# An empty half position in each gate chunk, and the last expert groups mixed straight from PSUM

## What is computed

```python
edge_index = jnp.stack([src, dst])
x = x + gnn(layernorm(x), edge_index, ...)            # attention over 212500 edges
x = x + ffn(layernorm(x)[None], ...)[0]
# ffn: gates from a graph attention over 131072 + 12500 edges, 4 heads x 4 experts
h = (x_flat @ W_gat).reshape(M, HEADS, NUM_EXPERTS)
alpha = softmax over the edges of a node of leaky_relu(a_src[src] + a_dst[dst], 0.2)
agg = segment_sum(h[src] * alpha[:, :, None], dst) + b_gat
scores = layernorm(agg, ln_gamma, ln_beta).reshape(M, HEADS, NUM_EXPERTS).mean(1)
w = softmax(top_k(scores, 2))
for ei in range(NUM_EXPERTS):
    hh = gelu(x @ W1[ei] + b1[ei], approximate=False)
    out = out + g[..., None] * (hh @ W2[ei] + b2[ei])
```

## Time and profile before

| | us |
|---|---|
| median of 3 runs | 5126.29 |
| lowest and highest of them | 5109.45, 5126.61 |
| profiled execution, its own time | 5112.58 |
| span of the profile, first to last instruction | 5110.8 |

### The profile page before, as it was taken

How to read it: one execution, slowest core, us unless ns; L and a number is a source line. 1 busy time by engine, 2 the same in 40 slices (tenths; PEclk the granted TensorE clock), 3 DMA queues, 4 the chain that set the end, 5 groups by cost and what they waited for, 6 DMA issues and landing times.

```text
span 5110.8 us, 56011 instructions
## 1 busy us (share of the span) xinstructions
PE 3488.7 (68%) x13829; PEld 2416.2 (47%) x13829; DVE 3343.7 (65%) x7445; ACT 2023.4 (40%) x5460; POOL 3027.1 (59%) x3037
## 2 busy tenths in 40 slices
PE   0443346566666665666665658898888988898995
PEld 0332223333333333333333328777766767676874
DVE  8988966666666666666555556265656666665478
ACT  0321145566565665566665656222222222221121
POOL 0000077777777777777777740777777777776001
PEclk9876677877888788787787875899999999999897
DMA  3111144333333333333444447322222222221079
GB/s 117 66 48 43 50 112 105 105 102 103 103 103 103 103 102 102 99 97 103 106 106 106 106 122 246 91 45 45 43 64 43 47 41 43 43 47 40 28 296 357
DMA packets 273867, 489.23 MB, mean 96 GB/s; under 512 B 78747, under 2 KB 174438, under 8 KB 267292
## 3 DMA queue, kind: packets, MB, share of 16 engines
q0 software_dynamic: 128928, 271.00, 22.2%
q1 hardware_dynamic: 144636, 214.78, 12.0%
HBM read 368.67 MB, written 116.87 MB: 95 GB/s over the span
## 4 chain that ended last, share of the span: by engine, by line
DVE 28%; PE 25%; POOL 24%; issue 12%; DVEq 5%; ACT 4%; DMA 2%; SPq 0%; POOLq 0%
POOL MEM L611 23%; PE ps L1606 16%; DVE MEM L1200 6%; DVEq L1187 4%; DVE MEM L864 2%; DVE MEM L866 2%; PE ps L1672 2%; PE ps L1660 2%; ACT hot L710 2%; POOL MEM L598 2%; PE ps L1636 1%; DVE MEM L877 1%; DVE MEM L1030 1%; DVE MEM L878 1%; PE ps L1548 1%
## 5 line engine op out<-in xcount | busy, mean ns | idle before, releaser
L598 POOL DMA_INDIRECT MEM<-h_table,MEM x1856 | 1818.5, 980 | 1171.7 <-DVE MEM L980 606.6
L1606 PE MATMUL ps<-MEM,hot 128*128 128x257 f32 x3712 | 1372.9, 485 | 367.4 <-DVE MEM L1200 293.7
L611 POOL DMA_INDIRECT MEM<-gate_table,FI x1122 | 1167.9, 1041 | 525.6 <-issue 341.6
L1200 DVE SCALAR_TENSOR_TENSOR MEM<-MEM,FI,ps 128x257 f32 x1856 | 894.3, 482 | 722.9 <-PE ps L1606 442.6
L1606 PEld LDWEIGHTS ps<-MEM,hot 128*128 128x128 f32 x3712 | 725.1, 228 | 958.8 <-ACT hot L710 521.1
L710 ACT ACTIVATE hot<-hot,FI 128x128 f32<-128x128 f32 x1856 | 889.1, 479 | 2.2
L689 ACT ACTIVATE hot<-iota_row,FI 128x128 f32<-128x128 f32 x1856 | 736.0, 397 | 372.6 <-PE ps L1606 348.7
L1660 PE MATMUL ps<-MEM 128*128 128x256 f32 x3136 | 768.3, 401 | 26.1 <-DMA MEM<-xT_tiles 26.1
L1672 PE MATMUL ps<-MEM 128*128 128x256 f32 x3136 | 743.0, 391 | 7.3 <-ACT MEM L750 7.3
L750 ACT ACTIVATE MEM<-ps,b_cols 128x256 f32<-128x256 f32 x784 | 324.6, 472 | 961.9 <-PE ps L1660 961.7
L1660 PEld LDWEIGHTS ps<-MEM 128*128 128x128 f32 x3136 | 616.7, 201 | 122.5 <-issue 22.2
(11 more groups left out here) (284 smaller groups left out, 3174.2 us busy)
## 6 DMA issues: line engine op xcount, KB each, us to landing
y_rows<-MEM SPq DMA_DIRECT2D x196, 256.0 KB, 2.1
MEM<-y_rows SPq DMA_DIRECT2D x49, 1024.0 KB, 7.6
MEM<-h_table,MEM POOLq DMA_INDIRECT x1856, 2.8
h_table<-MEM SPq DMA_DIRECT2D x196, 128.5 KB, 2.7
MEM<-gate_table,FI POOLq DMA_INDIRECT x1122
x_rows<-MEM SPq DMA_DIRECT2D x14, 896.0 KB, 6.7
xT_tiles<-MEM SPq DMA_DIRECT2D x14, 896.0 KB, 4.2
MEM<-xT_tiles SPq DMA_DIRECT2D x98, 128.0 KB
```

Source lines behind the costliest of these rows:

```text
L598: pool.indirect_dma_start(rings[c % 2][:, j, :], None, h_table, bass.IndirectOffsetOnAxis(ap=GI.bitcast(I32)[:, q:q + 1], axis=0)).then_in ...
L611: pool.indirect_dma_start(GR[:, c % GATE_RING, j, :], None, gate_table, bass.IndirectOffsetOnAxis(ap=FI.bitcast(I32)[:, q:q + 1], axis=0)) ...
L1200: dve.scalar_tensor_tensor(target, target, falls[:, p, j:j + 1], ps[:, at:at + ROW], ALU.mult, ALU.add).then_inc(added, 1)
L1606: pe.matmul(ps[:, at:at + ROW], hot[:, q % HOTS, :], rings[p][:, j, :], start=True, stop=True).then_inc(summed, 1)
```

## The change

`ITEMS` becomes 19: a chunk has one more half position, position 4, at which nothing is done, between step 3 and step 4. The steps behind it come half a slot later. Since 19 is odd, chunks with an even number have step 3 on half 0, and chunks with an odd number have it on half 1. `SUMS_AT` becomes 346 (slot 173), and the constants behind it follow: `MIX_LOADS_AT` 176, `SQRT_AT` 176, `TOP_AT` 179, `GATES_BY` 178, `MIX_FROM` 179, `LATE` 45.

Groups 0 to 44 go through `y_rows` and the mixes as before. Groups 45 to 48 (slots 180 to 195) don't: their x1 rows are loaded at slot 178, TensorE adds the bias b2 with one more matmul for each tile, and VectorE's `late_mix` adds the gated result from PSUM to the x1 rows in place of `y_copy`. `mixed_by` is capped by 45 and no longer by 37.

```diff
-ITEMS = 18
+ITEMS = 19
-MIX_LOADS_AT = (SUMS_AT + 12) // 2
+MIX_LOADS_AT = (SUMS_AT + 6) // 2
-MIX_FROM = (SUMS_AT + 14) // 2 + 1
+GATES_BY = (SUMS_AT + 10) // 2
+MIX_FROM = GATES_BY + 1
+LATE = -(-MIX_FROM // EXPERTS)
 def mixed_by(n):
-    return max(0, min((n - MIX_FROM + 1) * 3 // 2, GROUPS - 12))
+    return max(0, min((n - MIX_FROM + 1) * 3 // 2, LATE))
 def gate_item(position):
-    return (c, k) if 0 <= c < GATE_CHUNKS else (None, position - SUMS_AT)
+    return (c, k if k < 4 else k - 1 if k > 4 else None) if 0 <= c < GATE_CHUNKS else (None, position - SUMS_AT)
@@ SyncE @@
-                store_y(n)
+                if n < LATE * EXPERTS:
+                    store_y(n)
                 if n % 4 == 3 and g + 2 < GROUPS:
+                    sp.wait_ge(hid_ready, 4 * (n + 1))
                     load_xe(g + 2)
+                if n == GATES_BY:
+                    sp.wait_ge(top_ready, 1)
+                    for i, g_late in enumerate(range(LATE, GROUPS)):
+                        for t in range(2):
+                            sp.dma_start(x1_late[i][:, t, :], tile_of(x1_rows, 2 * g_late + t)).then_inc(late_in, 16)
@@ VectorE @@
+            def late_mix(n):
+                g, e = divmod(n, EXPERTS)
+                rows = x1_late[g - LATE]
+                if e == 0:
+                    dve.wait_ge(late_in, 32 * (GROUPS - LATE))
+                dve.wait_ge(y_ready, n + 1)
+                for z in range(2):
+                    if e:
+                        dve.wait_ge(dve_done, last_of[z])
+                    at = 2048 + n % 2 * 512 + z * D
+                    o = dve.scalar_tensor_tensor(rows[:, z, :], ps[:, at:at + D], gates[:, 2 * g + z, e:e + 1], rows[:, z, :],
+                                                 ALU.mult, ALU.add)
...
+                dve.engine_nop().then_inc(y_copied, 1)
-                        y_copy(n)
+                        (y_copy if n < LATE * EXPERTS else late_mix)(n)
-            for g in range(mixed, GROUPS):
+            for g in range(mixed, LATE):
                 mix(g)
@@ TensorE, outputs(n) @@
+                    late = n >= LATE * EXPERTS
+                    if late:
+                        ins = pe.matmul(ps[:, at + t * 256:at + (t + 1) * 256], ones_row[:, :], b2_all[0:1, n % 4, :],
+                                        start=False, stop=True)
```

More of the change, by code:

```diff
@@ L177, in gate_turn_buffers, with finish_order @@
     return order
-MIX_LOADS_AT = (SUMS_AT + 12) // 2
+MIX_LOADS_AT = (SUMS_AT + 6) // 2
 SQRT_AT = (SUMS_AT + 7) // 2
 TOP_AT = (SUMS_AT + 12) // 2
-MIX_FROM = (SUMS_AT + 14) // 2 + 1
+GATES_BY = (SUMS_AT + 10) // 2
+MIX_FROM = GATES_BY + 1
+LATE = -(-MIX_FROM // EXPERTS)
 def mixed_by(n):
-    return max(0, min((n - MIX_FROM + 1) * 3 // 2, GROUPS - 12))
+    return max(0, min((n - MIX_FROM + 1) * 3 // 2, LATE))
+def finish_order():
+    order, mixed = [], 0
+    for n in range(SLOTS):
+        if n >= LATE * EXPERTS and n % EXPERTS == EXPERTS - 1:
+            order.append(n // EXPERTS)
+        order += range(mixed, mixed_by(n))
+        mixed = mixed_by(n)
+    return order + list(range(mixed, LATE))
 def gate_item(position):
     c, k = divmod(position - FIRST_AT, ITEMS)
-    return (c, k) if 0 <= c < GATE_CHUNKS else (None, position - SUMS_AT)
+    return (c, k if k < 4 else k - 1 if k > 4 else None) if 0 <= c < GATE_CHUNKS else (None, position - SUMS_AT)
 def program(nc, a, out, consts):
@@ L323, in program @@
         fin_ready = sem("fin_ready")
+        late_in, late_out = sem("late_in"), sem("late_out")
         fin_out = [sem(f"fin_out{s}") for s in range(MIX_RING)]
@@ L407, in program @@
         yin = [v[:, 0:2048].rearrange("p (e t d) -> p e t d", e=EXPERTS, t=2) for v in mix_bufs]
+        x1_late = [R1[:, 19040 + 512 * i:19040 + 512 * (i + 1)].rearrange("p (t d) -> p t d", t=2) for i in range(GROUPS - LATE)]
         x1in = [v[:, 2048:2560].rearrange("p (t d) -> p t d", t=2) for v in mix_bufs]
@@ L565, in _ @@
                         mixes += 1
-                while n >= MIX_LOADS_AT and mixes < mixed_by(n) + MIX_RING and mixes < g - 1:
+                if n == GATES_BY:
[3 more added lines that the diff above has]
+                            sp.dma_start(x1_late[i][:, t, :], tile_of(x1_rows, 2 * g_late + t)).then_inc(late_in, 16)
+                while n >= MIX_LOADS_AT and mixes < min(mixed_by(n) + MIX_RING, LATE) and mixes < g - 1:
                     load_mix(mixes)
                     mixes += 1
-            for g in range(mixes, GROUPS):
+            for g in range(mixes, LATE):
                 load_mix(g)
@@ L613, in _ @@
                                             ).then_inc(gate_landed[c % GATE_RING], 16)
-            for g in range(GROUPS):
-                s = g % MIX_RING
-                pool.wait_ge(fin_ready, 2 * (g + 1))
+            for i, g in enumerate(finish_order()):
+                rows, signal = (x1in[g % MIX_RING], fin_out[g % MIX_RING]) if g < LATE else (x1_late[g - LATE], late_out)
+                pool.wait_ge(fin_ready, 2 * (i + 1))
                 if g < GROUPS - 1:
-                    pool.dma_start(out[2 * g * P:2 * (g + 1) * P, :].rearrange("(t p) d -> p t d", p=P),
-                                   x1in[s]).then_inc(fin_out[s], 16)
-                else:
-                    pool.dma_start(out[(TILES - 2) * P:(TILES - 1) * P, :], x1in[s][:, 0, :]).then_inc(fin_out[s], 16)
-                    pool.dma_start(out[(TILES - 1) * P:, :], x1in[s][0:LAST, 1, :]).then_inc(fin_out[s], 16)
+                    pool.dma_start(out[2 * g * P:2 * (g + 1) * P, :].rearrange("(t p) d -> p t d", p=P), rows).then_inc(signal, 16)
+                else:
+                    pool.dma_start(out[(TILES - 2) * P:(TILES - 1) * P, :], rows[:, 0, :]).then_inc(signal, 16)
+                    pool.dma_start(out[(TILES - 1) * P:, :], rows[0:LAST, 1, :]).then_inc(signal, 16)
             for s in range(MIX_RING):
-                pool.wait_ge(fin_out[s], 16 * (GROUPS // MIX_RING + (s < GROUPS % MIX_RING) + (s == (GROUPS - 1) % MIX_RING)))
+                pool.wait_ge(fin_out[s], 16 * (LATE // MIX_RING + (s < LATE % MIX_RING)))
+            pool.wait_ge(late_out, 16 * (GROUPS - LATE + 1))
         @block.scalar
@@ L769, in _ @@
                     if c is not None:
-                        gate_step(c, k)
+                        if k is not None:
+                            gate_step(c, k)
                 if n == SQRT_AT:
@@ L1468, in mix @@
                             fins.add(o)
+            last_of = {}
+            def late_mix(n):
[10 more added lines that the diff above has]
+                                                 ALU.mult, ALU.add)
+                    if e < EXPERTS - 1:
+                        last_of[z] = done.add(o)
+                    else:
+                        fins.add(o)
+                dve.wait_ge(dve_done, done.n)
+                if e == EXPERTS - 1:
+                    dve.wait_ge(fin_ready, fins.n)
+                dve.engine_nop().then_inc(y_copied, 1)
             values = gate_values()
@@ L1673, in outputs @@
                                         hidT[:, n % 2, f, t * P:(t + 1) * P], w2[:, 4 * (n % 4) + f, :],
-                                        start=f == 0, stop=f == 3)
+                                        start=f == 0, stop=f == 3 and not late)
+                    if late:
+                        ins = pe.matmul(ps[:, at + t * 256:at + (t + 1) * 256], ones_row[:, :], b2_all[0:1, n % 4, :],
+                                        start=False, stop=True)
                 ins.then_inc(y_ready, 1)
```

## The result

The changed kernel takes 5111.51 us, the median of 9 runs (5109.31 to 5117.56); the kernel before, run on the same chip, 5126.61 (9 runs, 5109.45 to 5134.12). The ratio is 0.9973, with a 95% interval of 0.9963 to 0.9984: by the ratio a gain of 14 us, where I had forecast 5080. The time fell inside my case "within 0.5%", but not by its mechanism.

A forecast was written before the change was run, and what follows sets the result against it. GpSimd's gathers were taken to bound the kernel, 176.1 us a pair against 174.5 of compute. Folds 4 us later, TensorE's end at 4994.5 and 21 mixes gave span 5070, time 5080, range 5055 to 5114.

The forecast's parts named there:

- within 0.5%: Case that the whole time changes by no more than a measurement can tell, about 25.6 us; chance 0.17.
- The bound, and the base of 82.9 us: Middle stage: gathers set 88.06 us a chunk, compute engines alone 82.90, so a chunk may lengthen up to the gathers' pace.
- The even chunk: Step 3 on half 0: waits of 1.6 and 2.3 us, VectorE's first add 0.7 us later than before.
- the batches then run at VectorE's pace: Behind the first batch in a chunk, VectorE was taken to set the pace, so delays were counted at its first add.
- t0: Start of the count within a chunk: step 3, at 3402.44 in chunk 1 of the kernel before.
- The odd chunk: Step 3 on half 1: TensorE stands 8.3 us for gelu, runs a slow half, first add 8.0 us later than before.
- The first rival: Odd chunks become the bound; a pair above 176.1 us adds its excess eight times, time 5156 at 185; chance 0.07.
- The folds: Behind step 1 of chunk 16: 0.7 us for that chunk, folds end 4 us later, 4837.8 in place of 4833.8.
- The bias: Late slots on TensorE: 32 bias matmuls at 0.216 us, 6.9 us in all, bounds 0 and 13.
- The end: Behind the folds: TensorE ends at 4994.5, 21 mixes of 66.6 us are left, span 5070 against 5110.8.
- The transfers: Rival: from slot 179 on, 60 MB of ring loads and stores bound the end, time about 5100; chance 0.17.
- The rule on the table load: ScalarE: a table switch drains about 1.38 us more, making a pair 177.3 us and the end some 9 later; left out.

The follow-up runs named there:

- e_gap_only: Half of the changed kernel: 19 half positions with the empty one, but all 49 groups through y_rows and mixes; ratio 0.9970 to the kernel before, median 5100.8 us.
- even kind: Against the changed kernel: 18 half positions, the empty one ahead of step 4, step 3 always on half 0, all groups through the mixes; single run 5106.4 us.
- the later exponential: The changed kernel with ScalarE's exponential of step 3 one slot later, behind gelu(n + 1); ratio 0.9911 to the kernel before, median 5069.8 us.
- both repairs: The changed kernel with the exponential behind gelu(n + 1) and the late groups' bias on VectorE; ratio 0.9870 to the kernel before, median 5050.0 us.

## Why the prediction was wrong

**The bound, and the base of 82.9 us.** Right. The gathers were the bound, and a chunk's length against theirs was the thing to look at.

**The even chunk.** The chain to gelu held: 1.39 us of wait for the exponential and 2.42 us for gelu stand in chunk 2 where I had put 1.6 and 2.3. Its timeline (step 3, step 4, `outputs`, first batch):

```profile
3497.62 0.20 PE L1753 MATMUL ps<-ident,MEM 8*66 8x8 f32 x1
...
3506.34 0.47 PE L1758 MATMUL ps<-ident,MEM 66*128 66x66 f32 x4 [1.39 <-ACT MEM L782]
3509.22 5.33 PE L1721 MATMUL ps<-MEM 128*128 128x256 f32 x16 [2.42 <-ACT MEM L772]
...
3519.31 0.53 PE L1772 MATMUL ps<-MEM 128*60 128x128 bf16 x6 [0.91 <-DVE MEM L1307]
```

The failed step is "the batches then run at VectorE's pace". I measured the delay at VectorE's first add, where it is small, and carried 0.7 us; that add came at t0 + 22.4, 1.5 later than before. But the distance from TensorE's first batch to the next step 1 is 54.5 us before and after (3421.51 to 3476.03; 3519.31 to 3573.85), and 54.1 to 54.9 in chunks 1 to 15 of the changed kernel: TensorE's own arrival is what moves the rest. It comes at t0 + 21.7, not + 19.07, 2.6 us later.

**The odd chunk.** The wait (8.19 us, forecast 8.3) and the slow half behind it held too:

```profile
3406.22 0.19 PE L1753 MATMUL ps<-ident,MEM 8*66 8x8 f32 x1
...
3418.28 6.42 PE L1721 MATMUL ps<-MEM 128*128 128x256 f32 x16 [8.19 <-ACT MEM L772]
...
3434.19 0.53 PE L1772 MATMUL ps<-MEM 128*60 128x128 bf16 x6 [1.89 <-DVE MEM L1307]
```

The first batch is at t0 + 28.0, 8.9 later than before, where I carried 8.0. The pair is so 165.8 + 2.6 + 8.9 = 177.3 us and not 174.5. With the delays of VectorE's first add in their place (1.5 and 8.3) it would be 175.6, still below the gathers, so it is the choice of the engine that fails. From chunk 5 on the parts shift, 3.6 to 3.9 us in even chunks and 7.6 to 8.0 in odd ones, and the sum stays near it. The margin I had left was 1.6, so 2.8 us in the pair turned the sign: TensorE was 8.9 us behind the gathers of before at chunk 3 (3573.85; 3565.00) and, losing another 9.3 in the 13 chunks from there, 18 us behind at chunk 16, 15 after my number. The first rival named just this mechanism, but I had priced its harm from 176.1 on with 0.07 for a loss and nothing for the part between; the odds went to the wrong place.

**The folds.** From step 1 of chunk 16 to their end it took 129.2 us, before 124.0; I had 0.7 more, and it was 5.1: 3.8 up to the first fold (4727.95 to 4810.75; before 4709.75 to 4788.73), 3.2 of it by the first batch, and 1.3 in the folds, where the granted clock is 0.71 and was 0.73. With that the folds end 19 us after my 4837.8.

**The bias.** A term of the sum that was mis-sized: 6.9 us, bounds 0 and 13; it was 25 to 26. I divided `outputs`, 3.45 us, by the 16 rows of the trace and called that a matmul. But `outputs` issues 8 matmuls (my "16 matmuls" in the part on the kernel are rows too), and each of them makes two rows; so does the bias one, "x2" for one matmul. At 0.43 us each it would be 14 us. Measured were 0.63 us for each of the two bias matmuls of a slot and 0.29 more on the other 8 of its `outputs`: (5.00 - 3.45) x 16 = 25 us; with 0.09 more on `hidden` beside it the slot as a whole is 1.64 x 16 = 26. The timeline of before had the same "x2" for a single matmul with one row of weights (L1684, once a chunk, 0.43 us at 3389.17), and I did not count. What made the price 0.63 and not 0.43 is not shown.

**The end.** The other terms of the end held. 21 mixes were left and took 66.59 us (66.6), the wait for `xT_tiles` is gone, the last gate came 43.0 us behind the folds (44.5), the first mix behind it, and a `late_mix` cost 0.9 us and was hidden. The mixes waited once, 4.54 us, for the late x1 rows, as foreseen. Against 5070: 19 for the folds, 17 for TensorE's slots (the bias 19, the rest 2 less), 2 for the last mixes being late: 38 us, the measured difference.

**The transfers.** As a rival they were wrong for the changed kernel, where 248 to 333 GB/s were moved in the stretches of 20 us from 4910 us to TensorE's end. For e_gap_only, with the transfers busy for 0.92 to 1.03 of the time from 4940 us on, they were right in kind and small in size: VectorE waited 4.3 us for them.

**The rule on the table load.** What the prediction cites from the Trainium skill, "ScalarE: Activation LUTs", section "What ACT_TABLE_LOAD costs", would by the same estimate have made a pair 177.3 us, which is what was measured, but for another reason: in chunk 1 of the changed kernel the load, 1.28 us long, starts 0.02 us behind the exponential, and the gelu 0.02 us behind the load, as before. No run here shows a drain.

**The 14 us.** The two profiles differ by 2.4 us, the runs on that chip by 14. The second profile of the kernel before, of another stretch, is 7.8 us above the changed one. The profiles explain the smaller numbers only; where the kernel before loses the rest on that chip stays open.

## What to carry to other kernels

A wait that is filled on one engine has to be followed into the queues of all the others: here the exponential that TensorE no longer waited for was still what ScalarE's queue stood on, and the gelu behind it became the new wait; putting the long wait behind the work that is ready (three lines) was worth more than the whole change. When a version differs in several constants, give each a run of its own before the gain is put down to the one that the change was made for. When an interval is lengthened up to another engine's pace, carry the delay from the engine whose distance to the next interval is constant, and do not trust a margin smaller than the error of the count. And before a row's mean is used as the price of an instruction, count how many rows one instruction leaves.

## What the runs showed that I had not expected

The pace of the gathers is not a constant of the kernel. Nothing about them was changed, and a chunk of 66 took 88.06 us before, 88.77 in the even kind, 87.02 with the later exponential and 86.77 with both repairs. A gather takes 0.94 us, and some take up to 2.15. Between 3600 and 4400 us of the kernel before 62 of 599 take over 1.2 us. Of these 38 lie beside a VectorE instruction of 1.2 us or more, and the other 24 beside the one-hots (L1284, 0.95 us); each of the 9 instructions of L1364 and the 9 of L1367 has such a slow gather beside it. But 52 of the 525 gathers of at most 1.0 us lie beside a long instruction as well, so length alone does not decide it. GpSimd's timeline, while VectorE works on chunk 12:

```profile
4369.96 0.94 POOL L611 DMA_INDIRECT MEM<-gate_table,FI  x1 [0.30 <-issue]
4371.21 1.98 POOL L611 DMA_INDIRECT MEM<-gate_table,FI  x1 [0.30 <-issue]
...
4378.88 2.14 POOL L611 DMA_INDIRECT MEM<-gate_table,FI  x1 [0.30 <-issue]
4381.32 1.97 POOL L611 DMA_INDIRECT MEM<-gate_table,FI  x1 [0.30 <-issue]
```

VectorE begins instructions of 1.23 us (L1346) at 4371.14 and of 1.53 us (L1364, L1367) at 4378.48 and 4380.93. Between 3600 and 4400 us the gathers' time above 0.945 us adds up to 49.7 us before, 55.5 in the even kind and 41.1 with the later exponential: 1 us a chunk less in the last, as its pace. VectorE has the same work in them, at other times against the gathers. That the instructions hold up the gathers is a reading from where they lie; no run took them away.
